# Order of work in a 16-head attention loop: a PSUM copy ahead of exponentials, a turn ahead of a projection, an addition ahead of maxima

## The reference, cut to what matters

```python
def _L0_attn_ref(x, qkv_w, qkv_b, out_w, out_b, decay_alpha):   # 16 heads of 8 features, T = 256
    qkv = x @ qkv_w.T + qkv_b
    q, k, v = ...
    logits = jnp.einsum('bhqd,bhkd->bhqk', q, k) / SCALE
    logits = logits - alpha[:, None, None] * dist[None]         # alpha = softplus(decay_alpha), dist = |i - j|
    attn = jax.nn.softmax(logits, axis=-1)
    out = jnp.einsum('bhqk,bhkd->bhqd', attn, v)
    out = out.transpose(0, 2, 1, 3).reshape(B, T, D)
    return out @ out_w.T + out_b
x = x + _L0_attn_ref(_layernorm(x), ...)
x = x + 0.5 * _L0_ffn_ref(_layernorm(x), ...)                   # the layer that follows
```

## Time and profile before

| What | Value |
|---|---|
| median of three runs | 1364.35 us (1364.29 to 1367.82) |
| the profiled execution's own time | 1367.0 us |
| its span (first to last instruction) | 1365.2 us |
| attention loop in it | from about 409 us to about 588 us |
| TensorE busy over the span | 1193.8 us (87%) |
| VectorE busy | 964.7 us (71%) |
| ScalarE busy | 847.8 us (62%) |
| GpSimd busy | 823.5 us (60%) |
| granted TensorE clock, mean | 0.959 of full speed |

### The profile page before, as it was taken

One profiled execution on the slowest core, in us unless ns is written; L12 is line 12 of the kernel. 1 busy time (PEld: TensorE's weight loads), 2 busy tenths in 40 slices (PEclk: granted clock), 3 DMA queues, 4 the chain that ended last, 5 costly groups with the idle time before them and its releaser, 6 DMA issues. The chain is left out here.

```text
span 1365.2 us, 36481 instructions
## 1 busy us (share of the span) xinstructions
PE 1193.8 (87%) x12629; PEld 883.0 (65%) x12630; DVE 964.7 (71%) x2520; ACT 847.8 (62%) x2470; POOL 823.5 (60%) x872
## 2 busy tenths in 40 slices
PE   4899898999888888969998999989879867889994
PEld 2567685766755555536776767768479854648984
DVE  5899768998766666769996699968844346674334
ACT  2899858998544444459997689984435534234552
POOL 5899638998454343159994589954167741117772
PEclk9999999999989999999999999999879998878998
DMA  6001100011000000000111001113157740017764
GB/s 211 20 21 25 35 10 19 21 25 25 21 11 3 3 3 3 3 1 17 25 25 28 16 9 24 31 27 79 31 169 228 206 141 0 1 31 212 225 205 133
DMA packets 71571, 79.26 MB, mean 58 GB/s; under 512 B 26791, under 2 KB 52070, under 8 KB 71270
## 3 DMA queue, kind: packets, MB, share of 16 engines
q1 hardware_dynamic: 65765, 65.49, 16.9%
q0 software_dynamic: 5632, 11.55, 3.2%
HBM read 55.52 MB, written 8.91 MB: 47 GB/s over the span
## 5 line engine op out<-in xcount | busy, mean ns | idle before, releaser
L853 POOL TENSOR_TENSOR rnp<-ss,mhalf 128x16 f32<-128x16 f32 x64 | 186.3, 2912 | 21.1 <-DVE ss L703 20.1
L2085 DVE SCALAR_TENSOR_TENSOR act_b<-bank,vec,gl 128x128 f32<-128x128 f32 x264 | 76.7, 345 | 136.7 <-ACT gl L1908 106.7
L1824 PE MATMUL bank<-arena 128*128 128x128 f32 x1056 | 138.7, 283 | 1.7 <-issue 0.8
L1824 PEld LDWEIGHTS bank<-arena 128*128 128x128 f32 x1056 | 129.2, 197 | 6.0 <-issue 3.7
L2129 POOL DMA_INDIRECT arena<-u_rows,inv_u x88 | 86.6, 984 | 74.6 <-DVE inv_u L2056 44.0
L785 ACT ACTIVATE pA<-bank,nb,rn 128x128 f32<-128x128 f32 x256 | 113.3, 464 | 12.6 <-DVE nb L714 12.6
L785 ACT ACTIVATE pB<-bank,nb,rn 128x128 f32<-128x128 f32 x256 | 113.3, 462 | 10.5 <-DVE nb L714 10.2
L848 POOL TENSOR_TENSOR arena<-arena 128x512 f32<-128x512 f32 x64 | 104.7, 1636 | 14.5 <-DVE arena L678 14.3
L1908 ACT ACTIVATE gl<-bank,vec 128x128 f32<-128x128 f32 x264 | 77.9, 366 | 54.0 <-PE bank L1824 39.2
L1599 DVE TENSOR_REDUCE act_b<-bank 128x2 f32<-128x512 f32 x128 | 79.5, 685 | 39.3 <-PE bank L1482 39.3
L2135 POOL DMA_INDIRECT y_rows<-stg,inv_u x88 | 86.5, 983 | 33.8 <-issue 20.4
(11 more groups left out here) (332 smaller groups left out, 3253.9 us busy)
## 6 DMA issues: line engine op xcount, KB each, us to landing
arena<-in_L_ffn_We SPq DMA_DIRECT2D x88, 384.0 KB
arena<-arena SPq DMA_DIRECT2D x64, 128.0 KB, 2.3
arena<-in_L_ffn_We SPq DMA_DIRECT2D x3, 768.0 KB, 7.3
arena<-U SPq DMA_DIRECT2D x32, 64.0 KB
u_rows<-U SPq DMA_DIRECT2D x2, 1024.0 KB, 5.2
U<-y_rows SPq DMA_DIRECT2D x8, 256.0 KB, 4.5
uT<-y_rows SPq DMA_DIRECT2D x8, 256.0 KB, 4.8
arena<-U SPq DMA_DIRECT2D x32, 63.5 KB
```

What stands on the lines that cost most here:

```text
L853: pool.tensor_tensor(rnp[:, :], ss[:, 1, :], mhalf[:, :], ALU.pow).then_inc(s.rn_self, 1)
L1824: m = pe.matmul(bank[q % 2][:, j * P:(j + 1) * P], we1[q][:, half * HR + j * P:half * HR + (j + 1) * P], xT[:, q, :], start=True, stop=True)
```

## The change

Three orders are changed; no instruction is added or removed but waits.

- TensorE, at n % 4 == 3: `xe_turned` stands ahead of `out_proj`. It gets the wait for `a_oTs` that `out_proj` has too, since both it and `o_back` write AS[2].
- VectorE, at n % 4 == 0: `added` is parted in two. The addition to x (L1629) stands right behind `result`, ahead of the maxima of n + 1; the moments stay behind these maxima.
- ScalarE: `o_turned_out` (n % 4 == 2) and `xe_out` (n % 4 == 3) stand ahead of the second pair of exponentials.

```diff
@@ aa_pe, step
                 if n % 4 == 2 and n > 4:
                     o_back(n // 4 - 1)
+                if n % 4 == 3 and n > 8:
+                    pe.wait_ge(s.a_oTs, n // 4)
+                    xe_turned(pe, 1, n // 4 - 2, AS[2])
                 if n % 4 == 3 and n > 4:
                     out_proj(n // 4 - 1)
-                if n % 4 == 3 and n > 8:
-                    xe_turned(pe, 1, n // 4 - 2, AS[2])
@@ aa_dve, added
                 dve.scalar_tensor_tensor(xb, U[:, 2 * b:2 * b + 2, :], COEF[2], xb, ALU.mult, ALU.add)\
                     .then_inc(s.x_new, 1)
+
+            def moments(b):
                 dve.wait_ge(s.x_new, NBATCH + b + 1)
                 xe_moments(dve, 1, b)
@@ aa_dve, step
                 if n % 4 == 0 and n > 4:
                     result(n // 4 - 2)
+                    added(n // 4 - 2)
                 if n + 1 < NA:
                     maxima(n + 1)
                 if n % 4 == 0 and n > 4:
-                    added(n // 4 - 2)
+                    moments(n // 4 - 2)
@@ aa_act, step
-                if n < NA:
-                    exps(n, 1)
                 if n % 4 == 2 and n > 4:
                     o_turned_out(n // 4 - 1)
                 if n % 4 == 3 and n > 8:
                     xe_out(act, 1, n // 4 - 2, AS[2])
+                if n < NA:
+                    exps(n, 1)
```

## The result

The changed kernel took 1357.0 us in the median of six runs (1356.12 to 1358.72); the kernel before, run beside it, 1366.09 (1362.5 to 1368.74). The ratio is 0.9937, with a 95% interval of 0.9923 to 0.9951, so 0.6% faster, 8.6 us. A second comparison on another chip, where both kernels are slower, gave 0.9955 (0.994 to 0.9969), 6.4 us. The forecast was 1358.2 and -6.2 us.

The account below looks back on a forecast made before the run. TensorE was taken to lead the attention part, with holes from hand-overs between engines. The terms -4.26 + 0.3 - 3.63 + 0.05 + 1.31 gave -6.2 us, 1358.2 us against the median 1364.35, range 1354.0 to 1364.0.

Parts of the forecast that it names:

- The floor and its steps: Attention loop, maxima to maxima: an undisturbed step takes 4.70 us; a middle sequence would read about 4.7, 4.7, 5.25, 6.45.
- The copy: ScalarE's copy of the turned rows ahead of the second exponentials: six steps of 5.96 gain 0.71 us each, -4.26.
- The turned sequence: Step of 6.49, turn before projection, copy before exponentials: 0 gained, as L1623 still ends the wait; extra wait entry 0.06 x 5, +0.3.
- the bound of 0.3: Step of 6.49: most that could be gained there, 0.3 us, if TensorE's second wait entry is passed for free.
- The addition: VectorE's L1629 ahead of the maxima: 0.66 us gained in four middle sequences, 0.99 in the first, 0 in the last; -3.63.
- The time to spare: VectorE, before the maxima: the moved L1629 would end at 501.54, maxima began at 501.98, so 0.4 us to spare.
- The first sequence: First sequence with a result: no turned rows ahead of it, so spare time near nothing; a cost of +0.05 us.
- The tail: Last sequence, steps 30 and 31: second exponentials wait behind the copies and nothing hides it; +0.55 + 0.76 = +1.31 us.
- The sum: Whole kernel: all terms together, -6.2 us, giving 1358.2 us from the earlier median of 1364.35.
- VectorE kept out at the seam: Rival: L1629 waits through back-to-back GpSimd strip operations, 5 x 3.95 = +19.8 us; about +13.5 in all, 1378; chance 0.06.
- Moments held by strips: Rival: VectorE's moments wait until the second L1706 ends, half of 3.6 us is lost, 1360 us; chance 0.10.
- Gain handed back or not readable: Rival: TensorE's clock falls elsewhere or a later part is bound by something else; 1361 to 1364 us; chance 0.22.

Follow-up runs that it names:

- short strips: The kernel before, with GpSimd's strip operations cut from 256 to 8 columns from the third sequence on; ratio 0.9983 to the kernel before.
- the copy alone: The kernel before, with only ScalarE's copy of the turned rows (`o_turned_out`) put ahead of the second exponentials; ratio 0.9961.
- the addition alone: The kernel before, with only the addition to x put ahead of the maxima on VectorE; ratio 0.9976.

## Why the prediction was right, point by point

- **The floor and its steps.** 4.7, 4.7, 5.25 and 6.45 were named; 4.7, 4.7, 5.20 and 6.35 were measured. The 6.45 was reckoned from the one sequence with 6.49; from the 6.40 of the others it would have been nearer.
- **The copy, -4.26.** Measured -4.56, six steps of 0.76 instead of 0.71. ScalarE still ended the wait, the scores stood 0.11 behind the copy, and no turned scores waited for exponentials in the middle sequences. The 0.05 is the copy itself: 0.38 us instead of 0.42.
- **The turned sequence, 0 and +0.3 for a wait entry.** The zero was right and for its reason: the copy comes 0.65 us ahead of the result's addition, and the scores start the same 0.23 behind that addition. The 0.3 between them was read from the one step with 0.32; in the other four it was 0.23, so there was less to gain than the bound of 0.3. The term of +0.06 a sequence had the wrong sign: the steps lost 0.05 each, and 0.13 in the one with the 6.49, -0.3 in all. No cost of the extra wait entry was seen.
- **The addition, -3.63.** Measured 0.66 in three middle sequences, 0.58 in the one with the 6.49, 0.99 in the first: -3.55. The runs show both halves of the reason, that GpSimd's operation holds it (0.42 us with short strips) and that VectorE gets in at the seam. The time to spare was 0.3 us, not 0.4. The moments were not held, as taken.
- **The first sequence, +0.05.** 6.07 both times, so nothing.
- **The tail, +1.31.** Measured +1.55 (9.75 against 8.20). The order is worth 1.36 of it, by the two kernels that differ in nothing else (9.75 and 8.39): 0.50 for the copy of step 30, where 0.55 was taken (8.88 with the copy alone, 8.39 with the addition alone), and 0.86 for the one of step 31, where 0.76 was taken (9.06 and 8.20). The other 0.19, and 0.17 in the step ahead (4.87 instead of 4.70), come with some kernels and not with others: the last step reads 4.87 or 4.88 in 8 of the 12 traces of other kernels than before, that with the addition alone among them. In those 8 the turn of the maxima (L1516) in step 30 starts 0.36 us behind their end, in the others 0.07. The three kernels that were traced twice, on two chips each, read the same both times. What delays it is not explained. That the tail's cost is carried into the next layer was right for 95 us, for the two copies together; beyond that it stays open.
- **The sum, -6.2.** The trace's account is -6.7, the times -8.6 and -6.4. That 1358.2 lies only 1.2 us from the 1357.0 measured is in part luck: the median it starts from, 1364.35, is of three runs, that of six is 1366.09, and the gain in time was 2.4 more than forecast.
- **The rivals.** VectorE kept out at the seam: no, L1707 was the one that got longer. Moments held by strips: no. Gain handed back or not readable: the gain was readable. What is not readable are the parts of 1 to 2 us, the tail's among them, and a gain in the later layers (above) is not ruled out.

## What to carry to other kernels

When two waits of a queue end within 0.02 us of each other, a list of waits names one of them, and taking that one away gains nothing: look at what else ends there before moving work. Move an operation that another engine can hold up into a gap that it fits at its longest, and read its longest from where that engine's operation ends, not from its mean. A reordering made for a steady loop can be paid for in the last passes, where nobody waits for what was brought forward and somebody waits for what was put back; here that was 1.36 us of the trace, too little for the times to show.

## What the runs showed of the hardware that was not expected

- A VectorE addition with both inputs in SBUF, 0.42 us alone, ends 0.28 us behind the end of the strip operation of GpSimd that it meets, wherever in it it comes: 60 additions in 12 traces came 0.53 to 1.19 us into an operation of 2.35, and all ended 0.28 to 0.29 behind it. The addition read 1.46 to 2.11 us by the place alone. The strip operation behind it takes the delay, 2.08 us instead of 1.89. The moments (one input) in the same place are not touched.
- Not every GpSimd operation holds it. The last addition of the kernel before runs inside L853, which raises 128x16 numbers to a power, and takes its 0.43 us, as if alone (timelines of GpSimd and VectorE):

```profile
595.42 2.94 POOL L853 TENSOR_TENSOR rnp<-ss,mhalf 128x16 f32<-128x16 f32 x1
...
596.21 0.43 DVE L1629 SCALAR_TENSOR_TENSOR X<-U,X 128x256 f32<-128x256 f32 x1
```

- Where a further wait entry stands in TensorE's queue behind the one that ends last, it takes 0.22 to 0.23 us from that end to the next weight load (478.83 to 479.05, 495.43 to 495.66); where none stands behind it, 0.11 to 0.12 (489.19 to 489.30, and 454.92 to 455.04 before). In one sequence of four traces it took 0.32 instead, among them both traces of the kernel before, in the same sequence; that is not explained.
- The same program took 46 us longer on another chip, all of it in the two mixtures of experts, where weights stream from HBM at 170 instead of 212 GB/s, and nothing in the attention loop.
